# In units 9, 17 and 19 of a batch, dt*u is scaled by B on ScalarE and transposed back on TensorE

## The reference, cut to what matters

```
def step(hst, inp):
    dt_t, B_t, C_t, u_t = inp
    dA = jnp.exp(dt_t[..., None] * A)
    dBu = dt_t[..., None] * B_t[:, None, :] * u_t[..., None]
    hst = dA * hst + dBu
    y = jnp.einsum('bdn,bn->bd', hst, C_t)
    return (hst, y)
```

## Time and profile before

| | |
|---|---|
| median of three runs | 2734.17 us (2731.04 to 2740.05) |
| the profiled execution | 2753.53 us |
| its span, first to last instruction | 2751.6 us |
| mean granted TensorE clock | 0.967 of full speed |
| VectorE's 512 scans of the Mamba mixer | first start 757.6 us, last start 2524.3 us |
| busy, whole span | PE 2466.9 us, DVE 2244.3, ACT 1961.6, POOL 1899.4 |

### The profile page before, as it was taken

How to read it: one execution, slowest core, us unless ns; L and a number is a source line. 1 busy time by engine, 2 the same in 40 slices (tenths; PEclk the granted TensorE clock), 3 DMA queues, 4 the chain that set the end, 5 groups by cost and what they waited for, 6 DMA issues and landing times. The chain is left out here.

```text
span 2751.6 us, 42267 instructions
## 1 busy us (share of the span) xinstructions
PE 2466.9 (90%) x15334; PEld 1916.0 (70%) x15334; DVE 2244.3 (82%) x2324; ACT 1961.6 (71%) x2841; POOL 1899.4 (69%) x1213
## 2 busy tenths in 40 slices
PE   5999998699698999999999999999999999977894
PEld 4888886566266767777677777776777777766563
DVE  6788886454189999899998998999999999997554
ACT  3656565266589788788787888978879889773562
POOL 1211212232289999999999998988989989897562
PEclk9999999799899999999999999999999999999897
DMA  1211212422323033041330421303303113051133
GB/s 53 65 50 50 64 46 79 99 78 66 91 86 112 29 127 122 21 132 51 97 120 21 134 82 51 124 10 115 117 9 124 67 58 116 21 166 46 61 105 127
DMA packets 143233, 219.62 MB, mean 80 GB/s; under 512 B 27076, under 2 KB 109892, under 8 KB 143044
## 3 DMA queue, kind: packets, MB, share of 16 engines
q1 hardware_dynamic: 134884, 194.84, 22.5%
q0 software_dynamic: 8160, 22.29, 2.9%
HBM read 174.56 MB, written 42.53 MB: 79 GB/s over the span
## 5 line engine op out<-in xcount | busy, mean ns | idle before, releaser
L1521 POOL TENSOR_TENSOR m_state<-m_state,m_c_all 128x1024 f32<-128x1024 f32 x512 | 1199.0, 2364 | 125.2 <-DVE m_state L1628 122.9
L1628 DVE TENSOR_TENSOR_SCAN m_state<-m_decay,m_ps_d 128x1024 f32<-128x1024 f32 x512 | 1152.0, 2274 | 92.1 <-ACT m_decay L1687 46.3
L1687 ACT ACTIVATE m_decay<-m_dt,m_aneg 128x511 f32<-128x511 f32 x1024 | 663.9, 709 | 20.1 <-DVE m_state L1628 19.4
L1965 PEld LDWEIGHTS m_ps_d<-m_bdiag,m_duT 128*128 128x128 f32 x4096 | 497.6, 194 | 96.3 <-issue 74.2
L1978 PE MATMUL m_ps_y<-k_ident,m_state 128*128 128x128 f32 x4096 | 521.0, 274 | 6.6 <-POOL m_state L1521 6.5
L1965 PE MATMUL m_ps_d<-m_bdiag,m_duT 128*128 128x128 f32 x4096 | 509.2, 278 | 17.0 <-DVE m_state L1628 16.4
L1978 PEld LDWEIGHTS m_ps_y<-k_ident,m_state 128*128 128x128 f32 x4096 | 468.4, 142 | 66.9 <-issue 55.8
L1616 DVE TENSOR_TENSOR m_ps_d<-m_ps_u,m_b_all 128x1024 f32<-128x1024 f32 x256 | 315.6, 1233 | 34.7 <-DMA m_b_all<-m_bc_rows 14.2
L1872 PE MATMUL m_ps_f<-k_w_2a,k_w_1b 128*128 128x512 f32 x512 | 255.8, 625 | 43.2 <-ACT m_up L1784 30.9
L1897 PE MATMUL m_ps_f<-m_up,k_w_1b 128*128 128x512 f32 x512 | 230.2, 592 | 0.7 <-ACT m_up L1784 0.7
L280 POOL TENSOR_TENSOR a_trig_lo<-a_trig,a_trig_hi 128x2048 fp32r<-128x2048 f32 x16 | 75.6, 4724 | 160.7 <-ACT a_trig_hi L561 160.7
(11 more groups left out here) (228 smaller groups left out, 4318.8 us busy)
## 6 DMA issues: line engine op xcount, KB each, us to landing
m_c_all<-m_bc_rows SPq DMA_DIRECT2D x128, 512.0 KB, 5.7
m_b_all<-m_bc_rows SPq DMA_DIRECT2D x64, 512.0 KB, 7.4
out<-m_xw SPq DMA_DIRECT2D x32, 512.0 KB, 3.3
a_w_2a<-x SPq DMA_DIRECT2D x16, 512.0 KB, 4.6
a_xres<-x SPq DMA_DIRECT2D x16, 512.0 KB, 5.4
x<-a_xout SPq DMA_DIRECT2D x16, 512.0 KB, 3.3
k_w_2a<-x SPq DMA_DIRECT2D x16, 512.0 KB
m_xw<-out SPq DMA_DIRECT2D x16, 512.0 KB, 8.6
```

The costliest lines, as they stand in the source:

```text
L1521: nc.gpsimd.tensor_tensor(s, s, c_all[:, n, :, :], ALU.mult).then_inc(weighed, 1)
L1628: nc.vector.tensor_tensor_scan(state[:, r, :, :].rearrange("p n t -> p (n t)"), decay[:, r, :, :].rearrange("p n t -> p (n t)"), ps_d[i % ...
L1687: ins = nc.scalar.activation(decay[:, r, j, 1:S], dt_sb[:, c % DR, 1:S], ACT.Exp, scale=aneg[:, c, n:n + 1])
L1965: ins = nc.tensor.matmul(ps_d[1][:, j, t * P:(t + 1) * P], duT[:, c % DR, t, :], bdiag[:, n // 2, TT * j + t, :], start=True, stop=True)
```

## The change

ScalarE scales `duT` of the unit's channel block by B, eight activations of 128 x 128 with a scale for each partition (time), into a new buffer `du_b`. It does so at its position 7 for unit 9, 14 for unit 17 and 17 for unit 19, behind the `softplus` and `silu` of that position. TensorE then transposes the eight blocks back in place of the eight products with `bdiag`. There is one buffer: each scaling waits until the drive before it that uses `du_b` is done. `drive` of these units waits for `du_b_ready`. All other odd units stay as they are, and `bdiag` is still made.

```
+    SCALED = {9: 7, 17: 14, 19: 17}
+    scaled_units = sorted(SCALED)
...
+        du_b = sb("du_b", [P, 2 * TT, P])
...
+            def scale_duT(st, unit):
+
+                h, b, at = st.half(0), st.item(0), scaled_units.index(unit)
+                c, n = unit // NP, unit % NP
+                act.wait_ge(bt_ready, b + 1)
+                act.wait_ge(duT_ready, CT * b + c + 1)
+                if at:
+                    act.wait_ge(drive_full, UN // 2 * b + scaled_units[at - 1] // 2 + 1)
+                elif st.has(-1):
+                    act.wait_ge(drive_full, UN // 2 * b - UN // 2 + scaled_units[-1] // 2 + 1)
+                for j in range(2):
+                    for t in range(TT):
+                        ins = nc.scalar.activation(du_b[:, TT * j + t, :], duT[:, c % DR, t, :], ACT.Copy,
+                                                   scale=bt[h][:, 2 * n + j, t:t + 1])
+                ins.then_inc(du_b_ready, 1)
...
                     if i == 23 and st.has(1):
                         softplus(st, 1, 0)
+                    for unit in scaled_units:
+                        if SCALED[unit] == i and st.has(0):
+                            scale_duT(st, unit)
...
+                at = scaled_units.index(i) if i in SCALED else None
+                if at is not None:
+                    pe.wait_ge(du_b_ready, len(scaled_units) * b + at + 1)
...
                 for j in range(2):
                     for t in range(TT):
-                        ins = nc.tensor.matmul(ps_d[1][:, j, t * P:(t + 1) * P], duT[:, c % DR, t, :],
-                                               bdiag[:, n // 2, TT * j + t, :], start=True, stop=True)
+                        if at is not None:
+                            ins = nc.tensor.transpose(ps_d[1][:, j, t * P:(t + 1) * P],
+                                                      du_b[:, TT * j + t, :], id_sb[:, :])
+                        else:
+                            ins = nc.tensor.matmul(ps_d[1][:, j, t * P:(t + 1) * P], duT[:, c % DR, t, :],
+                                                   bdiag[:, n // 2, TT * j + t, :], start=True, stop=True)
```

More of the change, by code:

```diff
@@ L1278, in mamba @@
         b_made = [sem(f"b_made{m}") for m in range(NP // 2)]
+        du_b_ready = sem("du_b_ready")
         scaled = sem("scaled")
```

## The result

The changed kernel takes 2914.44 us (median of four runs, 2913.04 to 2916.58), the kernel before 2734.06 us beside it (four runs). The ratio is 1.0659, with a 95% interval of 1.0643 to 1.0675: 180 us slower. The forecast was 2915 us.

The account below looks back on a forecast made before the run. No engine alone bounds the kernel; the bound passes from queue to queue. Eight batches at 11.9 us (95), seven at 11.8 (83) and the last (3) add 181 us to 2734.2: 2915 us, range 2850 to 2945.

Parts of the forecast that it names:

- Both stalls: TensorE waits for ScalarE's scaled blocks: 3.77 us before drive 17, and drive 19 starts 9.4 us late.
- the clock's first share: Clock loss behind the stall before drive 17, after DT3's room: 1.3 us a batch, 0.6 in the first eight.
- The shift reaches X: From the copy of X on, all engines stand 8.5 us later, with no slack to make it up.
- The clock: TensorE's clock falls behind both stalls: 1.3 us (0.6 in the first eight batches) and 2.2 us a batch.
- rival A: Both stalls happen but the clock stays up: 133 us more, 2867 us; chance 0.17.
- Unit 9: Scaling hidden in ScalarE's wait for V1, drive 9 shorter: 0.2 us gain a batch, bounds 0 and 0.9.
- The last batch: No next convolution, so scaling 17 is in time; scan 19 later: 2.3 us, plus 1 for the clock.
- The first eight batches: Experts' weights on the path to drive 19 add 0.8 us; 11.9 us a batch in all, 95 us.
- B: Only one of the stalls reaches the end, some 4 us a batch: 60 us more, 2794 us; chance 0.07.
- C: Scalings run in ScalarE's idle time before V3, 0.90 us saved three times a batch: 2691 us; chance 0.04.
- D: Transposes don't keep TensorE's clock up, low from drive 17 to X: 3042 us; chance 0.04 with any longer loss.
- E: Nothing changes, ScalarE's idle time being where it is needed: 2734 us; chance 0.02.

Follow-up runs that it names:

- filled kernel: The whole change, but TensorE makes the unit's products over again in its stalls before drives 17 and 19, then waits for the scaled blocks: 2865.1 us.
- the kernel that only scales: The change with all three scalings made on ScalarE, but TensorE neither waits for nor reads them and makes all drives as before: 2816.8 us.

## Why the prediction was right, step by step

*Both stalls.* TensorE was to stand still 3.8 us before drive 17 and 5 us or more before drive 19. It stood still 3.71 and 5.63. From the SiLU of V3 to drive 17 and to drive 19 I had 4.45 us (2262.48 to 2266.93) and 16.2 us (to 2278.7). The profile has 4.54 and 17.02 us. The 0.8 us of difference are the softplus of block 3, which now waits 0.71 us for DT3: the clock's first share, forecast as 1.3.

*Batch 13 is not the common case.* In 12 of the 15 batches the clock stayed low for longer behind the first stall than in batch 13 (the others are 0 and 10). Batch 14, by stretch and in the timelines of TensorE and ScalarE:

```profile
2526.70:2533.50 6.80, 5.38 (x20) 4.27 (x21) 2.29 (x1) 4.99 (x11) 0.98 (x1) 0.50 0.00 0
```

```profile
2531.56 1.92 PE L1951 MATMUL m_ps_f<-k_x,m_wdt 97*128 97x512 f32 x2
```

```profile
2533.51 0.60 ACT L1707 ACTIVATE k_x<-m_ps_f 128x512 f32<-128x512 f32 x1 [1.82 <-PE m_ps_f L1951]
```

DT3 itself ran at half speed, and the softplus waited 1.82 us for it; in batches 1 to 7, where the experts' weights cover part of that, it waited 1.0. I had put the first share at 1.3 and 0.6, so it was undersized. In batch 14 the copy of X is 13.1 us late and the batch 12.6 us longer, both more than forecast.

*The shift reaches X; in part it is made up.* In batch 13 the copy of X comes 2432.84 - 2403.12 = 29.72 us after the SiLU of V3, where it came 18.35 us after it: 11.4 us late. The forecast without unit 9's gain was 8.5 + 1.3 + 2.2 = 12.0. The batch as a whole is 120.45 - 109.61 = 10.8 us longer; forecast 11.8. The 0.6 us between 11.4 and 10.8 were won elsewhere in the batch, most of it at unit 9, below. The filled kernel shows the stalls alone, since its clock doesn't fall there. From the SiLU of V3 to the copy of X it takes 27.70 us in batches 1 to 7 and 26.90 in batches 8 to 14, against 18.35: 9.35 and 8.55 us late, where I had 9.3 and 8.5. So the path over both stalls, and the 0.8 us of the experts' weights, were right. But its 15 batches are only 119 us longer than before, and I had 131 for them. "I see no slack in which they would make it up" was wrong by some 12 us: about 16 of 135 us are made up behind X, where I had 3, for unit 9.

*The clock.* Filling the stalls gave back 49 us; rival A had the time at full clock at 2867 us, measured 2865.1. That agreement is luck in part. In the 15 batches the filled kernel is 53 us ahead of the change (1785 and 1838 us), where the forecast had 47: the clock was undersized by 6 us, and the slack that I had put at nothing gave back 12. In the last batch the filling has no first stall to fill, and there the filled kernel is 2 us slower. The terms rest on two rows of before and a choice between bounds. (The prediction calls 1.88 us half of 3.60; half is 1.80. Four such matmuls do take 1.88 us in a row at full clock, so the 1.7 us stand.) The share behind drive 19, in batch 13: transposes, `add_up` and O start at 2420.14 and `add_up` 17 after them at 2425.68, 5.54 us for what took 0.88 + 0.87 + 1.73 = 3.48 at full clock. That is 2.1 us, against 2.2. In batch 14 the same takes 6.18 us (2541.71 to 2547.89), 2.7 more than at full clock.

*Unit 9*: forecast 0.2 us a batch, measured 5 us over 16 batches, 0.3, with an interval of 0.2 to 0.5. Batch 13 with unit 9 alone takes 109.1 us in place of 109.6 (from scan 0 to scan 0), so it is 0.5 there. Scan 9 waits 0.32 us for its drive in place of 1.24 (batch 13 of the changed kernel, batch 14 before).

*The last batch.* From its first scan to scan 19 it takes 2654.23 - 2588.51 = 65.7 us in place of 63.1: 2.6 us more, forecast 2.3 and up to 1 for the clock. But to its last scan it is 5.6 us more, and I had 3 in all: scan 19 is followed by a wait of 1.5 us for O behind the late drive 19, and the last scan waits 1.4 us behind a drive 31 that took 3.46 us in place of 2.05.

*The first eight batches.* They became 91 us longer (894 to 985 us), forecast 95; the next seven 81 us (772 to 853), forecast 83.

*The rivals.* B (one stall alone counts) is out: with either alone the time is 68 or 126 us up. C (faster) is out: TensorE does wait. The kernels with one of the units scaled ahead of the SiLU come nearest to it, and they aren't faster either (all three units at such places weren't run). Its price of 0.90 us for each unit was wrong, since a shorter drive 17 or 19 has nobody waiting for it. D (transposes don't keep the clock up) is out for this kernel: with unit 17 alone, ahead of the SiLU, TensorE has transposes alone from 2255.4 to 2258.0 of batch 13, at a granted clock of 1.00, and in the changed kernel the clock was back at full speed between the stalls of every batch. E (nothing) is 180 us off.

## What to carry to other kernels

Before work is moved to an engine that is "idle 15% of the time", ask where in its queue the idle time lies: the same eight activations cost 68 us behind the instruction that waits and nothing ahead of it. Then ask who waits for the part that gets shorter: of the places tried late in the batch, TensorE's 0.9 us shortened the scan's wait only in the drive ahead of the convolution that ScalarE and the scan were waiting for, and there by 0.9 us. A stall of a few microseconds on TensorE can cost more than its length, here 49 us in 180, through the clock that falls behind it. And one batch of a trace can be the exception: look at several before a term is called measured.

## What the runs showed of the hardware that I had not expected

TensorE's clock came back between the two stalls in all 15 batches. In batch 13 it was 1.00 from 2411 to 2417 and 0.50 again from 2417.5, in the middle of the second stall; DT3 and the first part of O (1.02 and 1.89 us) ran at full speed there. In batch 14 it was 0.50 up to 2533.5, so only the first part of O did (1.89 us).

The same stall doesn't always have the same price. With unit 17 alone, the clock fell behind a stall of 3.7 us in 11 of 15 batches and stayed at 1.00 in four. In the kernel that only scales, it fell behind a wait of 2.69 us in batch 13 and not in batch 11.

Useless work made a kernel faster: the 80 matmuls a batch that fill the stalls gave 49 us.
